# Moving three pieces of VectorE work in a four-layer transformer kernel: two operand splits to other slots, one row normalisation to GpSimd

## The reference

```python
x = x + _L0_xattn_ref(_layernorm(x, axis=-1), ctx_2048, ...)
x = x + _L0_ffn_ref(_layernorm(x, axis=-1), ...)
x = x + _L1_xattn_ref(_layernorm(x, axis=-1), ctx_2048, itok_BxS_0_1023, ...)
x = x + _L1_ffn_ref(_layernorm(x, axis=-1), ...)
...
def _div_clamp_fp8(x, scale):
    y = jnp.clip(x.astype(jnp.float32) / scale, -FP8_MAX, FP8_MAX)
    y = y.astype(jnp.bfloat16).astype(jnp.float32)
    return _fp8_roundtrip(y)
...
cat = jnp.concatenate([core, xout], axis=-1)
catq = _div_clamp_fp8(cat, proj_smooth)
return jnp.einsum('bsi,oi->bso', catq, wproj) * (proj_in_scale * proj_w_scale)
```

## Time and profile before

| | us |
|---|---|
| median of three runs | 870.1 |
| lowest, highest | 869.75, 871.5 |
| the profiled execution, its own time | 871.5 |
| its span in the profile | 869.4 |
| PE busy in the span | 811.9 (93%) |
| DVE, ACT, POOL busy | 665.3, 521.6, 466.3 |

### The profile page before, as it was taken

The page is one execution under the profiler, slowest core; times in us unless marked ns, Lnnn a source line. Parts: engine busy times, 40 slices in busy tenths (PEclk is TensorE's granted clock), DMA queues, the critical chain, the costliest instruction groups (busy, mean ns, idle before and its releaser), DMA issues.

```text
span 869.4 us, 14397 instructions
## 1 busy us (share of the span) xinstructions
PE 811.9 (93%) x4888; PEld 694.4 (80%) x4888; DVE 665.3 (77%) x1578; ACT 521.6 (60%) x1202; POOL 466.3 (54%) x782
## 2 busy tenths in 40 slices
PE   3677999999999999999899999999999999999998
PEld 2566788888888878888788787888888878777787
DVE  7978978899887998889888885955654758876633
ACT  6968777788678886787664645423322344656332
POOL 3665959779685996858852858431200027760000
PEclk9789999999999999999999999999999999999999
DMA  7000120011101030001000415847520010100001
GB/s 234 13 1 1 37 74 1 2 38 58 53 1 36 2 110 1 2 1 54 13 25 15 146 37 148 224 150 249 135 58 25 1 44 25 49 1 1 0 2 48
DMA packets 28376, 45.99 MB, mean 53 GB/s; under 512 B 3952, under 2 KB 18096, under 8 KB 28176
## 3 DMA queue, kind: packets, MB, share of 16 engines
q1 hardware_dynamic: 26800, 41.31, 16.1%
q10 hardware_dynamic: 1504, 3.77, 1.2%
HBM read 43.89 MB, written 1.18 MB: 52 GB/s over the span
## 4 chain that ended last, share of the span: by engine, by line
PE 63%; DVE 20%; ACT 7%; issue 3%; DMA 3%; POOL 3%; SPq 1%; ACTq 0%; DVEq 0%
PE PS L755 16%; PE PS L824 6%; PE PS L711 6%; PE PS L616 5%; PE PS L685 4%; PE PS L647 3%; PE PS L925 3%; PE PS L880 2%; PE PS L657 2%; DVE cat L1494 2%; PE PS L638 2%; PE PS L668 2%; POOL raw L2148 2%; DVE yb L1490 2%; PE PS L915 2%
## 5 line engine op out<-in xcount | busy, mean ns | idle before, releaser
L2148 POOL TENSOR_SCALAR raw<-raw,mvq,rsq 128x128 f32<-128x128 f32 x312 | 188.7, 618 | 9.4 <-DVE mvq L1635 7.9
L755 PE MATMUL PS<-xq,WH 128*128 128x512 f32 x480 | 151.1, 396 | 0.0
L755 PEld LDWEIGHTS PS<-xq,WH 128*128 128x128 f32 x480 | 88.0, 190 | 17.1 <-issue 0.8
L616 PE MATMUL PS<-WH,xq 128*128 128x256 f32 (+1 forms) x256 | 89.0, 366 | 8.2 <-DVE xq L1494 6.3
L755 PE MATMUL PS<-xq,WL 128*128 128x512 f32 x240 | 94.2, 392 | 0.0
L616 PE MATMUL PS<-WL,xq 128*128 128x256 f32 (+1 forms) x256 | 84.2, 348 | 0.0
L1081 ACT ACTIVATE P<-PS,sm 128x256 f32<-128x256 f32 x128 | 60.5, 489 | 36.0 <-DVE sm L1663 35.8
L824 PE MATMUL PS<-xq,m_hh 128*128 128x256 f32 x384 | 70.5, 283 | 4.7 <-DVE m_hl L1944 3.8
L1588 DVE BATCH_NORM_STATS2 st<-raw 128x6 f32<-128x128 f32 x320 | 72.0, 279 | 1.5 <-ACT raw L1053 1.0
L685 PE MATMUL PS<-PT,vr 128*128 128x256 f32 x256 | 67.9, 388 | 2.3 <-ACT PT L967 2.2
L711 PE MATMUL PS<-PH,cat 128*128 128x256 f32 x256 | 64.9, 293 | 5.4 <-DVE cat L1494 5.3
(11 more groups left out here) (299 smaller groups left out, 2222.6 us busy)
## 6 DMA issues: line engine op xcount, KB each, us to landing
wst<-in_wgu SPq DMA_DIRECT2D x24, 256.0 KB, 4.1
l_KM<-share SPq DMA_DIRECT2D x16, 384.0 KB, 3.9
wst<-in_wall SPq DMA_DIRECT2D x18, 256.0 KB, 3.1
l_KM<-share SPq DMA_DIRECT2D x16, 256.0 KB, 4.3
dst<-in_wdn SPq DMA_DIRECT2D x24, 128.0 KB, 3.6
wst<-in_wkvx SPq DMA_DIRECT2D x8, 256.0 KB, 3.2
l_KM<-share SPq DMA_DIRECT2D x16, 128.0 KB, 4.0
m_pre<-in_wo ACTq DMA_DIRECT2D x1, 2048.0 KB, 9.9
```

Of the source, the lines that this page charges most:

```text
L616: t = e.matmul(PS[:, b, o:o + n], xq[s][:, k, c * 128:(c + 1) * 128], W[:, k, w0:w0 + n], start=(k == 0 and i == 0), stop=(k == 1 and i == 1))
L755: t = e.matmul(PS[:, b, :], W[wi][:, gu, k, :], a[:, k, cols], start=(n == 0), stop=(n == 5))
L2148: t = e.tensor_scalar(v, v, mvq[:, par, n, 0:1], rsq[:, par, n:n + 1], ALU.add, ALU.mult)
```

## The change

Three things move. DVE's `load_p(gp, 0)` and `load_p(gp, 1)` of steps 5, 9 and 13 go from slot 0 to slot 2. DVE's `load_w(gp+1, WORDER[3])` goes from slot 0 of steps 2, 6 and 10 to slot 4 of steps 1, 5 and 9. The normalisation of `bb` = 2 is split between DVE and POOL as that of `bb` = 0 and 1 is, and POOL's wait for the normalisation of `bb` = 3, ahead of its first product of expert halves, is removed. PE's and ACT's order stays as it is.

```diff
@@ count of semaphores
-        guessed_m, xn_p, xn_m = count("guessed_m", range(2)), count("xn_p", range(2)), count("xn_m", (2, 3))
+        guessed_m, xn_p, xn_m = count("guessed_m", range(3)), count("xn_p", range(3)), count("xn_m", [3])
@@ tensor: xs(bb)
-                c = xn_p if bb < 2 else xn_m
+                c = xn_p if bb < 3 else xn_m
@@ vector: ln_m(bb)
-                if bb > 1:
+                if bb == 3:
                     weave(ln_steps(bb, 1, xn_m.sem))
                     return
@@ vector: the loop over (s, k)
-                if s in (5, 9, 13) and k == 0:
+                if s in (5, 9, 13) and k == 2:
                     load_p(gp, 0)
                     load_p(gp, 1)
-                if s % 4 == 2 and s < 12 and k == 0:
+                if s % 4 == 1 and s < 12 and k == 4:
                     load_w(gp + 1, WORDER[3])
@@ gpsimd: the loop over (s, k), and behind it
-                    if s in (14, 15) and k == 2:
+                    if s > 13 and k == 2:
                         norm_m(s - 14)
...
-            w.wait_ge(xn_m.sem, xn_m.at[3])
             for n, (j, h) in enumerate(pairs):
```

## The result

| | before | changed | ratio [95% interval] |
|---|---|---|---|
| first measurement, median us | 870.6 | 881.1 (880.8 to 881.6) | 1.0121 [1.0103, 1.0139] |
| repeated on another chip (`g1_changed_again`) | 868.9 | 881.8 (880.6 to 882.8) | 1.0144 [1.0124, 1.0164] |

The change costs 10.5 to 13 us. The forecast was 874.0 us, its range 871.2 to 876.3: slower was right, the size was not. One of the 75 later executions of the kernel before took 3454 us; no run explains it, and it is in none of the ratios. The profiled execution took 880.7 us around a span of 878.9, 9.5 us more than that of before.

The account below looks back on a forecast made before the run. From 60 to 464 us PE's own order of work was taken as the bound, with waits for DVE's `cat`. Terms 0.5 + 1.8 + 1.6 = 3.9 us on the median of 870.1 gave 874.0 us, range 871.2 to 876.3.

Parts of the forecast that it names:

- Part 1: Attention, load_p pair moved from slot 0 to slot 2 of steps 5, 9, 13: 0.5 us, bounds 0.2 and 1.74.
- some 0.8 us come back: Step 5: DVE's norm of (5,3), 1 us later, misses POOL's subtraction and returns some 0.8 us.
- if it stays at 0.7, they were hidden: Sign for both load moves: PE's cat wait at steps 5 and 9 grows to about 1.8 us, else they were hidden.
- contention gives back: Rival: shifted DVE work avoids POOL's at steps 5, 9 and bb=3; 871.2 to 872.4 us, chance 0.24.
- Step 13: DVE's 1.07 us wait before the maximum of (13,4) takes up all but 0.2 us of the load_p pair; nothing counted.
- Part 2: Attention, load_w moved to slot 4: 0.88 us onto cat at steps 5 and 9, 1.8 us; nothing at step 1.
- The bound of 2.4 us: Upper bound for the load_w move, taking in half a pair at step 1 too.
- Part 3: Start of experts, POOL normalises bb=2: PE waits 1.8 us for xn at L747, bounds 1.6 and 2.5 us.
- Part 4: POOL's products, no longer waiting for bb=3, start at 476.6 us over DVE's chain: 0.9 us, bounds nothing and 1.6.
- the 0.9 us for the chain of `bb`=3: DVE's fourteen instructions, under six POOL instructions up to 481.5, end at about 483.4; PE waits 0.9 us more.
- The relief of the table: Router chain on DVE: L1839 to L1843 take near 1 us instead of 3.8, since POOL's products are done early.
- the end of the wait at L799: PE no longer waits 1.07 us for the one-hot table, subtracted from the terms at the experts' start.

Follow-up runs that it names:

- e1_splits_p: The kernel before with only load_p(gp, 0) and (gp, 1) moved to slot 2 of steps 5, 9 and 13: 873.1 us, ratio 1.0048.
- e5_wait_kept: The changed kernel with POOL's wait for the normalisation of bb=3 put back: 874.8 us, ratio 1.0070 to the kernel before.
- g4_before_small_products: The kernel before with POOL's first four products each cut into quarters: 868.2 us, ratio 0.9993.
- e2_split_w: The kernel before with only load_w of WORDER[3] moved to slot 4 of steps 1, 5 and 9: 873.0 us, ratio 1.0056.
- e4_no_wait: The kernel before with only POOL's wait for the normalisation of bb=3 removed: 872.2 us, ratio 1.0026.
- e3_norm_pool: The kernel before with only bb=2 normalised by POOL, its wait for the normalisation of bb=3 kept: 869.7 us, ratio 1.0008.

## Why the prediction was wrong

Part 1: **the step "some 0.8 us come back" failed.** It took 0.5 us out of a possible 1.74. The attention of `e1_splits_p` shows 1.8, all of it. It does not show where the prediction looked for it, either: PE's wait for `cat` stays at 0.71 us at step 5, and the wait for P ahead of it, which the sum had left out, grows from 0.17 to 1.42. By its own sign ("if it stays at 0.7, they were hidden") part 1 would have passed for free. The return itself happened as described: the norm of (5,3), 1.57 us in the earlier trace rows, missed POOL's subtraction. But DVE's run as a whole was shifted, and another of its instructions fell under another of POOL's. DVE in the changed kernel:

```profile
201.03 1.74 DVE L1705 TENSOR_TENSOR PL<-l_kt,PH 128x512 fp32r<-128x512 f32 x1
...
206.56 0.74 DVE L1681 TENSOR_TENSOR P<-P,sm 128x512 f32<-128x512 f32 x1
```

The norm gained 0.83 us, and the piece at the run's start, 0.82 us before, lost 0.92: POOL's subtraction stood from 200.94 to 202.23. In `e1_splits_p` it is the next piece, 1.77 us instead of 0.68. The argument looked at the one collision that the trace of before shows and not at where the shifted instructions land. The *contention gives back* rival, on the same argument, is refuted; its own objection, that DVE begins the run with POOL in the midst of its pieces, was the right one.

Step 13, counted at 0.2 us: the wait for `cat` grew from 1.83 to 2.16 us, and one step on, at 438.03, there is a new wait of 0.95 us for P (0.94 in `e1_splits_p`). DVE's L1444 took 1.27 us there instead of 0.17: it was held under POOL's last query and two memsets, of which the second ended at 432.28 and L1444 at 432.30. In `e5_wait_kept` it took 0.17 us, and the wait for P is not there. From the third L583 to L747 of `bb`=1 it is 132.1 us in `g4_before_small_products`, 133.6 in `e1_splits_p` and 133.8 in the changed kernel: 1.5 to 1.7 us. The profiled execution of before hid this, at 133.9 us, because its clock was 0.66 from 415 to 420 us.

Part 2: right where it counted. The sum said 1.8 us at steps 5 and 9, the attention of `e2_split_w` shows 1.6. At step 1 it counted nothing, because PE showed no wait for `cat` there. In the profiled execution of before the clock had fallen (0.74 from 100 to 105 us), and PE was late, which hid what DVE had to spare. Of the six kernels without part 2 whose clock was high there, four wait 0.35 to 0.53 us for `cat` and two not at all; the seven with part 2 and a high clock wait 0.81 to 1.36 us. PE in `e2_split_w`:

```profile
108.30 0.39 PE L711 MATMUL PS<-PH,cat 128*128 128x256 f32 x1 [1.32 <-DVE cat L1494]
```

From PE's first wait of 0.5 us for ACT's `yT` (at 89 to 93 us) to the first L583 it is 28.3 to 28.4 us in six of the nine kernels without part 2 (`e1_splits_p` and `g4_before_small_products` among them) and 29.1 to 29.2 in seven of the nine with it: 0.8 us more, which the profiled execution of before (29.8 us) hid. The bound of 2.4 us, which was to take in half a pair at step 1, comes to 2.2 by its own terms; measured, steps 5 and 9 with step 1 make 1.6 + 0.8 = 2.4 us.

Part 3: 1.46 us of wait at L747, where 1.8 was forecast and 1.6 was the lower bound. A Newton step took 0.28 us, not 0.30: the 0.30 of the prediction is the step to the `xn` row, and not one between two Newton rows.

Part 4: **the 0.9 us for the chain of `bb`=3 failed by its count.** The wait was 2.40 us instead of 0.9, above the bound of 1.6. The mechanism was the right one, and the Trainium skill, "SBUF — State Buffer", section "SBUF: two separate sides", has it as an exclusive lock of the port pair; the chain of 7.9 us instead of 3.1, with ends that coincide with POOL's, agrees. The prediction saw six POOL instructions up to 481.5. In the changed kernel the sixth ended at 484.47, and eight of DVE's fourteen were through by then, as foretold. But there were eight POOL instructions, up to 487.9: the product n = 2 followed at once and held an instruction of 0.16 us for 1.21, and n = 3, after 0.84 us for ACT, lay under the two instructions that write `xn`, which took 1.68 us instead of 0.74. The relief of the table (three instructions 0.28, 0.29 and 0.29 us instead of 3.8 together) and the end of the wait at L799 came as foretold, with 0.86 us for the three where the estimate was near 1 us.

**What the sum had no term for is the clock: 3.1 us**, the largest single item. A row that could have warned was there: the kernel before has a granted clock of 0.69 in the very stretch. The prediction named two new waits of PE within 8 us and priced them as waits alone.

In the prediction's own terms, by the trace: parts 1 and 2 in the groups 3.4 (forecast 2.3), the wait for POOL's `xn` 1.5 (1.8), for DVE's 2.4 (0.9), waits gone behind it -1.3 (-1.1), clock 3.1 (none), steps 13 and 14 1.7 (none): 10.8 us, minus 1.7 us that the profiled execution of before lost at its own low stretch at 415 us. That leaves 9.1 of the 9.5 us measured.

Three things stay open. The medians of `e1_splits_p` and `e2_split_w` lie 2 us further above before than their attention does. Steps 13 and 14 give part 1 another 1.5 us and step 1 gives part 2 another 0.8, so the traces account for 3.3 and 2.4 us of 3.9 each. The losses of before that hid them (1.5 us ahead of 120 us, 1.7 us at 415) also fit its profiled execution, at 871.5 us, being slower than the 869.1 us of 74 later ones, but which of them an execution has can be read only in profiled ones. Against a kernel without these two losses the change would cost, as an estimate from the traces, 3.4 + 0.8 + 1.7 + 1.5 + 4.4 + 0.2 = 12.0 us, between the 10.5 and 12.9 of the two medians. The two clusters of `e4_no_wait` are not explained. And what makes the granted clock fall is not: it stayed at 1.00 behind the 1.46 us wait of `e3_norm_pool` and fell in the kernel before behind one of 0.22 us.

## What to carry to other kernels

Price a new wait of the TensorE engine twice, as a wait and as what follows if the granted clock falls behind it; a few idle matmuls in the wait, no longer than it is, gave 3.3 us back here. When VectorE work is shifted under GpSimd work, lay the whole shifted run against GpSimd's instructions; one collision that goes away in the old trace says nothing on the next. And read a stretch of low clock in the profile of before as noise that hides waits: the room that it seems to leave behind it is not there in the next execution.

## What the runs showed of the hardware

- After waits of 1.46 and 2.40 us with 6 us of work between, the granted clock was 0.50 to 0.61 for some 10 us, which cost 3.1 to 3.3 us more than the short low stretch that stands there with idle matmuls in the waits. After the 1.46 us wait alone (`e3_norm_pool`) it stayed at 1.00; in the kernel before it fell to 0.69 from 485 to 490 us behind a wait of 0.22. The price is shown, the trigger is not.
- A DVE instruction of 128x2, 0.17 us by itself, took up to 1.27 us and ended within 0.02 us of the POOL instruction that it had met. POOL's products in quarters, 3.39 us instead of 2.53 for two, went with a chain of twelve such instructions and two of 128x256 of 5.8 us instead of 7.9, and a kernel 4.3 us faster. In the kernel before, the same cut removed a wait of 1.07 us and changed the time by less than can be measured (0.9993 [0.9979, 1.0007]).
